# Attention scores as float32 products on row halves, operands placed by GpSimd, in a four-stage network on one core

## Chip, cores and metric

One NeuronCore of a Trainium2 chip. The metric is the device time of one execution in microseconds; less is better. The kernel is a single launch that runs a whole small network on 2048 tokens of 128 features in float32.

## The reference

Four stages run one after the other: a state-space block, a local transformer of two layers, a latent attention, and a mixture of experts, with normalisations between them. The change lies in the latent attention alone:

```python
h = (x - mu) * jax.lax.rsqrt(var + LN_EPS) * ln_scale + ln_bias
c_q = h @ w_down_q.T          # 64 latents
c_kv = h @ w_down_kv.T        # 64 latents
q = (c_q @ w_up_q.T)          # 16 heads of 64, the same for k and v from c_kv
q = _apply_rope_subspace(q, DR)
k = _apply_rope_subspace(k, DR)
scores = jnp.einsum('bhqd,bhkd->bhqk', q, k) * scale
attn = jax.nn.softmax(scores, axis=-1)
out = jnp.einsum('bhqk,bhkd->bhqd', attn, v)
out = out @ w_out.T + residual
```

Every head scores 2048 queries against 2048 keys, each of 64 numbers.

## The kernel before

`latent_attention` works on pairs of heads (8 pairs, `g`), chunks of 512 queries (4, `j`), the two heads of the pair (`w`) and row tiles of 128 queries (4, `r`). One row tile is a 128x2048 block of scores in four PSUM banks (`score`); there are 16 x 16 = 256 of them and one ahead of the loop. The loop body, unrolled for two pairs, runs four times on every engine; nothing but semaphores orders the engines.

TensorE does this for each row tile: the scores of the next row tile (`score_banks`, L1449), banks 0 and 1 once the exponential has read them, then banks 2 and 3; four transposes of probabilities (`turn_tiles`, L1468); in `r == 0` the output products (`output`, L1512); four value products (`mix`, L1500), which alternate between two column halves of the array; four more transposes; and with `w == 0`, `r == 1` and `r == 3`, a piece of the next pair's key and query projection (`pieces`, L1325), whose products alternate between two row halves of the array.

VectorE takes the maximum of each bank (`row_max`, L1479), joins them to `bias` (L1482) and turns half of the probabilities into 32x32 blocks (`turn_blocks`, L1546). ScalarE computes the exponentials, two banks at a time (`exps`, L1487), and copies transposes, outputs and pieces out of PSUM (L1472, L1508, L1520, L1464). SyncE writes the turned blocks to DRAM and reads them back (`write_blocks`, `read_blocks`). GpSimd adds outputs (`add_output`, L1528, L1532) and makes the next pair's operands (`make_parts`).

The scores are made as follows. A float32 number is split into a high part, rounded to the format fp32r, and the rest. `make_parts` multiplies a piece of 256 positions by cosines and sines (L1566), adds the two (L1569), rounds (L1577) and subtracts (L1579). For keys the parts lie in `k_part`, and `send_keys` moves them by four DMAs to `keys`, high parts on rows 0 to 63, low parts on rows 64 to 127. For queries they lie in `q_pair`, and `send_q` (L1339) copies a chunk of one head to both row halves of `q_unit`. Two fp32r passes over all 128 rows then give one bank of scores, one with the high and one with the low part of the queries as stationary operand.

The first pair is made in a block of its own ahead of the loop, from L1349 on: TensorE projects eight pieces of 512, VectorE multiplies (L1427), GpSimd adds (L1386), ScalarE rounds (L1442), VectorE subtracts (L1416), SyncE sends keys (L1371) and queries. In the same block SyncE fills `far` and `bounce` with zeros from `near`.

Of the kernel before, what the change touches and what calls it, by code (L numbers as in the profile page):

```python
# [6 lines left out]
F32 = mybir.dt.float32  # L7
# [1189 lines left out]
def latent_attention(nc, dram, const, x, acc):  # L1197
# [5 lines left out]
    with Space(nc, "g") as sp:  # L1203
# [5 lines left out]
        with Space(nc, "ga") as s:  # L1209
# [11 lines left out]
            with nc.Block() as block:  # L1221
# [71 lines left out]
        k_part = sp.sb("k_part", [P, 2, QH], F32R)  # L1293
# [4 lines left out]
        most = sp.sb("most", [P, 2, 4])  # L1298
        bias = sp.sb("bias", [P, 2])
        sums = sp.sb("sums", [P, 2, RT, 2])  # L1300
        zero = sp.sb("zero", [P, 1])
# [9 lines left out]
             ("w_loaded0", "w_loaded1", "first_full", "first_free", "roped", "high_ready", "low_ready", "k_loaded",  # L1311
              "q_loaded0", "q_loaded1", "score_done", "maxes", "bias_ready", "exp_done", "turn_done", "near_copied",
              "blocks_turned", "written0", "written1", "landed0", "landed1", "mix_done", "mixed_ready", "out_full",
              "out_taken", "added", "piece_full", "piece_taken", "raw_free", "order", "sums_added", "recip_ready",
              "near_read", "zeroed", "values_set", "rescaled")}
        q_loaded = [m["q_loaded0"], m["q_loaded1"]]
# [10 lines left out]
        def send_keys(sync, turn, at, half):  # L1327

            sync.wait_ge(m["low_ready"], PIECES + 2 * half + 1)
            cols = slice(at * QH, (at + 1) * QH)  # L1330
            for head in range(2):
                for part in range(2):
                    sync.dma_start(keys[part * 64:(part + 1) * 64, turn, head, cols].bitcast(F32),
                                   k_part[head * 64:(head + 1) * 64, part].bitcast(F32)).then_inc(m["k_loaded"], 16)

        def send_q(sync, head, chunk):

            for half in range(2):
                sync.dma_start(q_unit[half * 64:(half + 1) * 64, head].bitcast(F32),  # L1339
                               q_pair[head * 64:(head + 1) * 64, :, chunk * QW:(chunk + 1) * QW].bitcast(F32))\  # L1340
                    .then_inc(q_loaded[head], 16)
# [7 lines left out]
        k_first = probs[:, :, 2 * CH:].bitcast(F32R)  # L1349
        with nc.Block() as block:  # L1350

            @block.sync
            def _(sync):
# [13 lines left out]
                for c_ in range(NC):  # L1367
                    sync.wait_ge(m["low_ready"], 2 * c_ + 1)
                    for head in range(2):
                        for part in range(2):  # L1370
                            sync.dma_start(keys[part * 64:(part + 1) * 64, 0, head, c_ * CH:(c_ + 1) * CH].bitcast(F32),  # L1371
                                           k_first[head * 64:(head + 1) * 64, part, c_ % 2 * CH:(c_ % 2 + 1) * CH]
                                           .bitcast(F32)).then_inc(m["k_loaded"], 16)
                sync.wait_ge(m["low_ready"], PIECES)
                for w in range(2):
                    send_q(sync, w, 0)
# [741 lines left out]
```

## Time and profile before

| | us |
|---|---|
| median of 3 runs | 2464.31 (2462.95 to 2468.85) |
| the profiled execution | 2464.99 |
| its span, first to last instruction | 2462.8 |
| TensorE busy | 2126.8 |
| VectorE busy | 1676.6 |
| ScalarE busy | 1381.8 |
| GpSimd busy | 897.5 |

The median is of plain runs; the spans and durations below are of the profiled execution. "PE" is a TensorE product, "PEld" the load of its stationary operand, "DVE" VectorE, "ACT" ScalarE, "POOL" GpSimd, "SP" SyncE. Matmuls are pipelined, so that a row of products lasts longer than the time from its start to the start of the next row; block lengths are read from start to start. A float32 product leaves two records. Duration and start of every row are as recorded; an instruction that waits in the engine's queue is counted from when it runs.

### The profile page before, as it was taken

How to read it: one execution, taken by the hardware profiler on the slowest of the kernel's cores; microseconds unless marked ns; L12 is line 12 of the kernel's file. 1: busy time of each engine (PE TensorE's matmuls, PEld its weight loads, DVE VectorE, ACT ScalarE, POOL GpSimd, SP SyncE). 2: the span in 40 equal slices, each digit the busy share in tenths (PEclk: the TensorE clock that was granted, in tenths of full speed). 3: DMA queues.
4: the chain of work that ended last, by engine and by line, in shares of the span. 5: the costliest groups of instructions: out<-in, count | busy, mean ns of one | idle time of the engine just before them, and what ended most of it. 6: DMA issues, size and time to landing. Idle time of an engine off the chain costs nothing. (4 is left out here: it accounts for less than half of the span.)

```text
span 2462.8 us, 38107 instructions
## 1 busy us (share of the span) xinstructions
PE 2126.8 (86%) x11662; PEld 1309.8 (53%) x11662; DVE 1676.6 (68%) x3033; ACT 1381.8 (56%) x2802; POOL 897.5 (36%) x883
## 2 busy tenths in 40 slices
PE   4745699877984599999999999999999999997397
PEld 2532377435862255556555555555565555553244
DVE  5767766596666477777677777677776777774544
ACT  4233465255630277777677777677776777774121
POOL 0625543264420344443334434344443444433000
PEclk8878899898997699999999999999999999998598
DMA  1001000000001467776677767667776677764100
GB/s 31 1 1 57 1 2 12 20 1 1 2 12 48 154 220 230 239 240 228 215 227 234 247 225 238 211 229 242 233 234 222 222 235 239 232 231 146 36 1 18
DMA packets 224395, 345.61 MB, mean 140 GB/s; under 512 B 16993, under 2 KB 169697, under 8 KB 223905
## 3 DMA queue, kind: packets, MB, share of 16 engines
q1 hardware_dynamic: 224160, 342.86, 42.1%
q8 instruction: 102, 1.67, 0.3%
q14 instruction: 133, 1.08, 0.1%
HBM read 148.55 MB, written 136.31 MB: 116 GB/s over the span
## 5 line engine op out<-in xcount | busy, mean ns | idle before, releaser
L1479 DVE TENSOR_REDUCE g.most<-g_score 128x1 f32<-128x512 f32 x1028 | 639.3, 683 | 342.3 <-PE g_score L1449 341.8
L1487 ACT ACTIVATE g.probs<-g_score,g.bias 128x1024 f32<-128x1024 f32 x514 | 568.0, 1110 | 65.1 <-DVE g.bias L1482 53.7
L1449 PE MATMUL g_score<-g.keys,g.q_unit 128*128 128x512 f32 x2056 | 561.7, 413 | 25.8 <-DMA g.q_unit<-g.q_pair 11.9
L1472 ACT ACTIVATE g.near<-g_turned 128x512 f32<-128x512 f32 x512 | 305.2, 596 | 325.9 <-PE g_turned L1468 325.7
L1449 PEld LDWEIGHTS g_score<-g.keys,g.q_unit 128*128 128x128 f32 x2056 | 361.3, 190 | 145.6 <-ACT g.probs L1487 60.1
L1468 PEld LDWEIGHTS g_turned<-top.ident,g.probs 128*128 128x128 f32 x2048 | 234.1, 140 | 243.2 <-issue 208.1
L1546 DVE STREAM_TRANSPOSE g.blocks<-g.probs 128x1024 f32<-128x1024 f32 x256 | 318.9, 1246 | 31.4 <-DMA bounce<-g.blocks 16.1
L1468 PE MATMUL g_turned<-top.ident,g.probs 128*128 128x128 f32 x2048 | 321.4, 279 | 0.0
L1500 PE MATMUL g_mix_ps<-g.near,mid.y_tok 128*64 128x512 f32 x1056 | 257.4, 609 | 6.3 <-DMA g.far<-bounce 6.3
L1500 PE MATMUL g_mix_ps<-g.far,mid.y_tok 128*64 128x512 f32 x1056 | 255.2, 605 | 0.0
L1566 POOL TENSOR_TENSOR mid.y_tok<-mid.y_tok,g.waves 128x512 f32<-128x512 f32 x128 | 163.7, 1279 | 229.7 <-ACT mid.y_tok L1464 229.7
L1528 POOL TENSOR_TENSOR g.scaled<-g.scaled,g.recip 128x512 f32<-128x512 f32 x67 | 69.7, 1040 | 424.9 <-ACT g.scaled L1520 415.0
L1500 PEld LDWEIGHTS g_mix_ps<-g.near,mid.y_tok 128*64 128x64 f32 x1056 | 64.6, 137 | 103.8 <-issue 96.0
L1500 PEld LDWEIGHTS g_mix_ps<-g.far,mid.y_tok 128*64 128x64 f32 x1056 | 64.3, 136 | 99.4 <-issue 99.4
L1487 ACT ACTIVATION_READ_ACCUMULATOR g.probs<-g_score,g.bias 128x1 f32 x514 | 100.5, 195 | 0.0
L1577 POOL TENSOR_TENSOR g.k_part<-mid.y_tok,g.zero 128x256 fp32r<-128x256 f32 x64 | 39.2, 612 | 161.3 <-DMA g.keys<-g.k_part 154.9
L1569 POOL TENSOR_TENSOR mid.y_tok<-mid.y_tok 128x256 f32<-128x256 f32 x128 | 93.1, 727 | 10.0
L1532 POOL TENSOR_TENSOR top.x_tok<-top.x_tok,g.scaled 128x512 f32<-128x512 f32 x67 | 85.7, 1279 | 5.3
L1464 ACT ACTIVATE mid.y_tok<-g_side 128x512 f32<-128x512 f32 x128 | 77.3, 604 | 1.9
L865 POOL TENSOR_TENSOR lt1.probs<-lt1.probs,lt1.total 128x768 f32<-128x768 f32 x32 | 46.9, 1467 | 71.1 <-DVE lt1.total L920 71.1
L1512 PE MATMUL g_side<-g.mixers,g.mixed 128*128 (+1 forms) x536 | 71.8, 277 | 1.2 <-ACT g.mixed L1508 1.2
L865 POOL TENSOR_TENSOR lt0.probs<-lt0.probs,lt0.total 128x768 f32<-128x768 f32 x32 | 46.9, 1467 | 70.9 <-DVE lt0.total L920 70.9
(358 smaller groups left out, 3235.6 us busy)
## 6 DMA issues: line engine op xcount, KB each, us to landing
bounce<-g.blocks SPq DMA_DIRECT2D x256, 512.0 KB, 5.2
g.far<-bounce SPq DMA_DIRECT2D x256, 512.0 KB, 4.4
g.q_unit<-g.q_pair SPq DMA_DIRECT2D x132, 256.0 KB, 4.4
g.keys<-g.k_part SPq DMA_DIRECT2D x256, 64.0 KB, 3.5
g.far<-g.near SPq DMA_DIRECT2D x8, 512.0 KB, 5.5
lt.turns<-turns SPq DMA_DIRECT2D x1, 2048.0 KB, 8.1
g.waves<-g_waves SPq DMA_DIRECT2D x1, 2048.0 KB, 10.2
g.keys<-g.probs SPq DMA_DIRECT2D x16, 128.0 KB, 2.4
```

The source lines that it names most:

```text
L865: nc.gpsimd.tensor_tensor(p, p, total[:, slot].unsqueeze(2).broadcast_to([P, HH, KEYS]), ALU.mult).then_inc(m["probs_ready"], 1)
L1449: ins = nc.tensor.matmul(score[:, b], q[:, part], k_of(b), start=(part == 0), stop=(part == 1))
L1464: nc.scalar.activation(raw[:, kind], side[:, kind], ACT.Copy).then_inc(m["piece_taken"], 1)
L1468: ins = nc.tensor.transpose(turned[:, k * P:(k + 1) * P], probs[:, r % 2, t * P:(t + 1) * P], ident[:])
L1472: nc.scalar.activation(near[:, w, tiles, r * P:(r + 1) * P], turned[:].rearrange("p (t n) -> p t n", n=P), ACT.Copy).then_inc(m["near_copi ...
L1479: nc.vector.tensor_reduce(most[:, slot, k:k + 1], score[:, k], AX.X, ALU.max, negate=True)\
L1487: nc.scalar.activation(probs[:, slot, k * 2 * CH:(k + 1) * 2 * CH], score[:, 2 * k:2 * k + 2].rearrange("p b n -> p (b n)"), ACT.Exp, bias ...
L1500: ins = nc.tensor.matmul(out, values[:, t], moving, start=(t < 2), stop=(t >= T - 2))
L1532: nc.gpsimd.tensor_tensor(a, a, scaled[:], ALU.add).then_inc(m["added"], 1)
L1546: nc.vector.transpose(blocks[:, r % 2].rearrange("p j t c -> p t j c"), probs[:, r % 2, NEAR * P:].rearrange("p (t j a) -> p t j a", j=4, ...
L1566: nc.gpsimd.tensor_tensor(both, both, waves[:, at].rearrange("p s n -> p (s n)"), ALU.mult)\
L1569: nc.gpsimd.tensor_tensor(total, total, both[:, QH:], ALU.add).then_inc(m["order"], 1)
```

## The change

The score product becomes a float32 product over 64 rows. `keys` holds the key blocks 0 and 2 of a head on rows 0 to 63 and the blocks 1 and 3 on rows 64 to 127; `queries` holds each head's queries on both row halves, for this pair and the next. One row tile's scores are two pairs of products, one product of a pair on each row half. `make_parts` no longer splits: it multiplies, and then adds cosine and sine part straight into the place where TensorE reads them, on 64 rows at a time, with a shift by 64 rows where needed: two additions for a piece of keys, four for a piece of queries. All DMAs of keys and queries go, with `send_keys`, `send_q`, `q_loaded` and `k_loaded`. TensorE waits for the operands of the next pair once in a pair, for the last of its 16 pieces. `row_max` takes one maximum over two banks in place of one for each bank. In the first block VectorE adds the keys into place and GpSimd the queries; ScalarE has nothing to do there.

```diff
-        keys = sp.sb("keys", [P, 2, 2, S], F32R)
-        q_pair = sp.sb("q_pair", [P, 2, S], F32R)
-        q_unit = sp.sb("q_unit", [P, 2, 2, QW], F32R)
+        keys = sp.sb("keys", [P, 2, 2, S // 2])
+        queries = sp.sb("queries", [P, 2, 2, S])
...
+        def place_keys(engine, turn, head, at, width, first, second):
+
+            block, inside = divmod(at * width, CH)
+            cols = slice(block // 2 * CH + inside, block // 2 * CH + inside + width)
+            return engine.tensor_tensor(keys[block % 2 * 64:block % 2 * 64 + 64, turn, head, cols],
+                                        first[head * 64:head * 64 + 64], second[head * 64:head * 64 + 64], ALU.add)
+
+        def place_queries(engine, turn, head, half, at, width, first, second):
+
+            return engine.tensor_tensor(queries[half * 64:half * 64 + 64, turn, head, at * width:(at + 1) * width],
+                                        first[head * 64:head * 64 + 64], second[head * 64:head * 64 + 64], ALU.add)
...
-                for n in range(PIECES):
-                    pool.wait_ge(m["first_free"], 2 * n + 2)
-                    nc.gpsimd.tensor_tensor(cos_part[:, n % 2], cos_part[:, n % 2], sin_part[:, n % 2], ALU.add)\
-                        .then_inc(m["roped"], 1)
-                nc.gpsimd.memset(zero[:], 0.0)
+                for c_ in range(NC):
+                    pool.wait_ge(m["first_free"], 4 * c_ + 4)
+                    for crossed in range(2):
+                        pool.wait_ge(m["zeroed"], 1 + 4 * c_ + 2 * crossed)
+                        for head in range(2):
+                            place_queries(nc.gpsimd, 0, head, head ^ crossed, c_, CH, cos_part[:, 1], sin_part[:, 1])\
+                                .then_inc(m["zeroed"], 1)
+                    pool.wait_ge(m["zeroed"], 5 + 4 * c_)
+                    pool.sem_inc(m["q_first"], 1)
...
+                    if kind == 0:
+                        dve.wait_ge(m["first_free"], 2 * n + 2)
+                        for head in range(2):
+                            ins = place_keys(nc.vector, 0, head, c_, CH, cos_part[:, 0], sin_part[:, 0])
+                        ins.then_inc(m["k_first"], 1)
...
-        def score_banks(pe, banks, q, k_of):
-
-            for b in banks:
-                for part in range(2):
-                    ins = nc.tensor.matmul(score[:, b], q[:, part], k_of(b), start=(part == 0), stop=(part == 1))
-                ins.then_inc(m["score_done"], 1)
+        def score_pair(pe, pair, turn, head, chunk, r):
+
+            cols = slice(chunk * QW + r * P, chunk * QW + (r + 1) * P)
+            for odd in range(2):
+                rows = slice(odd * 64, odd * 64 + 64)
+                nc.tensor.matmul(score[:, 2 * pair + odd], queries[rows, turn, head, cols],
+                                 keys[rows, turn, head, pair * CH:(pair + 1) * CH], start=True, stop=True)\
+                    .then_inc(m["score_done"], 1)
...
-            for k in range(4):
-                dve.wait_ge(m["score_done"], 4 * before + k + 1)
-                nc.vector.tensor_reduce(most[:, slot, k:k + 1], score[:, k], AX.X, ALU.max, negate=True)\
-                    .then_inc(m["maxes"], 1)
+            for k in range(2):
+                dve.wait_ge(m["score_done"], 4 * before + 2 * k + 2)
+                nc.vector.tensor_reduce(most[:, slot, k:k + 1], score[:, 2 * k:2 * k + 2].rearrange("p b n -> p (b n)"),
+                                        AX.X, ALU.max, negate=True).then_inc(m["maxes"], 1)
...
             nc.gpsimd.tensor_tensor(both, both, waves[:, at].rearrange("p s n -> p (s n)"), ALU.mult)\
                 .then_inc(m["order"], 1)
             pool.wait_ge(m["order"], n + 1)
...
+            if kind == 0:
+                for head in range(2):
+                    place_keys(nc.gpsimd, turn, head, at, QH, first, second).then_inc(m["order"], 1)
+                    pool.wait_ge(m["order"], n + 2 + head)
             else:
+                for crossed in range(2):
+                    for head in range(2):
+                        place_queries(nc.gpsimd, turn, head, head ^ crossed, at, QH, first, second)\
+                            .then_inc(m["order"], 1)
+                    pool.wait_ge(m["order"], n + 3 + 2 * crossed)
+            pool.sem_inc(m["parts_ready"], 1)
...
                                         if w == 1 and j == NC - 1:
                                             on = 1 - turn
-                                            pe.wait_ge(m["k_loaded"], 256 + 512 * (g + 1))
+                                            pe.wait_ge(m["parts_ready"], 16 * (g + 1) + 2)
```

## Rows read from the trace of the kernel before

**Rows 1.** The page: busy time, share of the span and instructions of each engine

```profile
PE 2126.8 (86%) x11662; PEld 1309.8 (53%) x11662; DVE 1676.6 (68%) x3033; ACT 1381.8 (56%) x2802; POOL 897.5 (36%) x883
```

**Rows 2.** Stretches: length, busy time (instructions) of PE, PEld, DVE, ACT, POOL, clock, DMA

```profile
1000.00:1400.00 400.00, 395.57 (x2060) 235.30 (x2058) 290.58 (x475) 286.72 (x514) 166.54 (x186) 0.99 0.70 231
...
1480.88:1523.79 42.91, 42.91 (x227) 25.37 (x225) 31.84 (x52) 31.32 (x57) 18.02 (x21) 1.00 0.70 233
```

**Rows 3.** Waits in 860 to 2260: us in total, times, longest us

```profile
PEld g_score L1449 <- ACT g.probs L1487: 58.6, 190, 0.9
...
PE g_score L1449 <- DMA g.keys<-g.k_part: 0.8, 2, 0.4
```

**Rows 4.** Timeline of TensorE: start us, us, what, shapes, records

```profile
1506.49 0.66 PE L1468 MATMUL g_turned<-top.ident,g.probs 128*128 128x128 f32 x4
1506.90 2.10 PE L1449 MATMUL g_score<-g.keys,g.q_unit 128*128 128x512 f32 x8
1508.84 0.60 PE L1468 MATMUL g_turned<-top.ident,g.probs 128*128 128x128 f32 x4
1509.36 1.94 PE L1500 MATMUL g_mix_ps<-g.far,mid.y_tok 128*64 128x512 f32 x8
1511.23 0.66 PE L1468 MATMUL g_turned<-top.ident,g.probs 128*128 128x128 f32 x4
1511.82 1.14 PE L1325 MATMUL g_side<-g.c,g.w_up 64*128 64x256 f32 x8
1512.88 2.12 PE L1449 MATMUL g_score<-g.keys,g.q_unit 128*128 128x512 f32 x8
1514.84 0.60 PE L1468 MATMUL g_turned<-top.ident,g.probs 128*128 128x128 f32 x4
```

**Rows 5.** Timeline of VectorE and ScalarE behind the scores that start at 1506.90

```profile
1507.64 2.48 DVE L1479 TENSOR_REDUCE g.most<-g_score 128x1 f32<-128x512 f32 x4 [1.84 <-PE g_score L1449]
...
1510.35 1.11 ACT L1487 ACTIVATE g.probs<-g_score,g.bias 128x1024 f32<-128x1024 f32 x1 [0.29 <-DVE g.bias L1482]
1511.37 0.19 ACT L1487 ACTIVATION_READ_ACCUMULATOR g.probs<-g_score,g.bias 128x1 f32 x1
1511.46 1.10 ACT L1487 ACTIVATE g.probs<-g_score,g.bias 128x1024 f32<-128x1024 f32 x1
```

**Rows 6.** Timeline of TensorE, window 1511.80 to 1511.83 alone

```profile
1511.82 0.49 PE L1325 MATMUL g_side<-g.c,g.w_up 64*128 64x256 f32 x2
```

**Rows 7.** Timeline of all engines around the third row tile of a unit

```profile
1491.28 2.26 PE L1449 MATMUL g_score<-g.keys,g.q_unit 128*128 128x512 f32 x8
...
1492.65 0.60 ACT L1464 ACTIVATE mid.y_tok<-g_side 128x512 f32<-128x512 f32 x1
1493.34 1.27 POOL L1566 TENSOR_TENSOR mid.y_tok<-mid.y_tok,g.waves 128x512 f32<-128x512 f32 x1 [0.39 <-ACT mid.y_tok L1464]
1493.38 0.60 PE L1468 MATMUL g_turned<-top.ident,g.probs 128*128 128x128 f32 x4
```

**Rows 8.** Groups by form: what, shapes, count, busy us, mean ns of one, idle before

```profile
L1566 POOL TENSOR_TENSOR mid.y_tok<-mid.y_tok,g.waves 128x512 f32<-128x512 f32 x128 | 163.7, 1279 | 229.7 <-ACT mid.y_tok L1464 229.7
L1569 POOL TENSOR_TENSOR mid.y_tok<-mid.y_tok 128x256 f32<-128x256 f32 x128 | 93.1, 727 | 10.0
...
L707 DVE TENSOR_REDUCE la1.inverse<-lp1.square 128x16 f32<-128x1024 f32 x16 | 19.2, 1200 | 0.0
```

**Rows 9.** Timeline of the block that makes the first pair

```profile
807.39 1.89 DVE L1427 TENSOR_TENSOR g.probs<-g_score,g.waves 128x512 f32<-128x512 f32 x3 [0.94 <-PE g_score L1325]
808.44 2.49 POOL L1386 TENSOR_TENSOR g.probs<-g.probs 128x512 f32<-128x512 f32 x2
...
812.88 1.64 POOL L1386 TENSOR_TENSOR g.probs<-g.probs 128x512 f32<-128x512 f32 x1 [1.95 <-DVE g.probs L1427]
...
845.59 3.66 PE L1449 MATMUL g_score<-g.keys,g.q_unit 128*128 128x512 f32 x8 [11.86 <-DMA g.q_unit<-g.q_pair]
```

**Rows 10.** Timeline of TensorE at the loop's jump, one of three

```profile
1548.61 3.68 PE L1449 MATMUL g_score<-g.keys,g.q_unit 128*128 128x512 f32 x8 [3.88 <-issue]
```

More of the change, by code:

```diff
@@ L1325, in projected @@
             return nc.tensor.matmul(out, w_up[rows, turn, swap * P:(swap + 1) * P], c[rows, cols], start=True, stop=True)
[L1327 to L1331, printed above, removed]
-                for part in range(2):
[L1333 to L1341, printed above, removed]
+        def place_keys(engine, turn, head, at, width, first, second):
[6 more added lines that the diff above has]
+                                        first[head * 64:head * 64 + 64], second[head * 64:head * 64 + 64], ALU.add)
         def load_w(sync, turn, pair):
@@ L1366, in _ @@
                                    [:, 0:4 * RUN]).then_inc(written[w], 16)
[L1367 to L1376, printed above, removed]
                 for w in range(2):
@@ L1430, in _ @@
                             .then_inc(m["first_free"], 1)
-                    if n:
-                        rest(n - 1)
-                rest(PIECES - 1)
-            @block.scalar
-            def _(act):
-                for n in range(PIECES):
-                    kind, c_ = n % 2, n // 2
-                    act.wait_ge(m["roped"], n + 1)
-                    if kind == 0 and c_:
-                        act.wait_ge(m["k_loaded"], 64 * c_)
-                    nc.scalar.activation(first_part(n, 0), cos_part[:, n % 2], ACT.Copy)\
-                        .then_inc(m["high_ready"], 1)
-        def score_banks(pe, banks, q, k_of):
-            for b in banks:
-                for part in range(2):
-                    ins = nc.tensor.matmul(score[:, b], q[:, part], k_of(b), start=(part == 0), stop=(part == 1))
-                ins.then_inc(m["score_done"], 1)
+                    if kind == 0:
[10 more added lines that the diff above has]
+                    .then_inc(m["score_done"], 1)
         def pieces(pe, turn, at):
@@ L1461, in take_piece @@
         def take_piece(act, half, kind):
-            act.wait_ge(m["raw_free"], 2 * half + 1 + kind)
+            act.wait_ge(m["parts_ready"], 2 * half + 1 + kind)
             act.wait_ge(m["piece_full"], 2 * half + 1 + kind)
@@ L1558, in read_blocks, with make_parts @@
                            bounce[4 * w + r].rearrange("(i p x) -> p i x", i=4, p=P)).then_inc(landed[w], 16)
-        def make_parts(pool, g, j, at, half, kind):
-            n = 3 * (2 * half + kind)
+        def make_parts(pool, turn, at, half, kind):
             both = raw[:, kind]
-            total = both[:, 0:QH]
+            first, second = both[:, 0:QH], both[:, QH:]
+            n = 8 * half + 3 * kind
             pool.wait_ge(m["piece_taken"], 2 * half + 2 + kind)
@@ L1622, in _ @@
                 pool.sem_inc(m["added"], 1)
[L1623 removed]
+                pool.sem_inc(m["parts_ready"], 2)
                 with pool.Fori(0, PAIRS_G // 2) as i:
@@ L1641, in _ @@
             def _(pe):
-                pe.wait_ge(q_loaded[0], 32)
-                pe.wait_ge(m["k_loaded"], 256)
-                score_banks(pe, range(4), q_unit[:, 0, :, 0:P], lambda b: keys[:, 0, 0, b * CH:(b + 1) * CH])
+                for k in range(2):
+                    score_pair(pe, k, 0, 0, 0, 0)
                 mix(pe, 0, range(0, 4))
```

75 lines of the change are left out of this document (18 added, 57 removed).

## The prediction

> **What bounds the kernel now.** I read the page's engine line first [rows 1]: TensorE is busy for 86% of the span, the other engines for 68% and less. A share is an average, so the stages came next [rows 2]. In the latent attention loop TensorE is busy 395.6 of 400 us at a granted clock of 0.99, VectorE 291, ScalarE 287, GpSimd 167. The reader is to see two things there: the loop is TensorE's, and the DMA share of 0.70 is large but belongs to an engine set that nobody waits for. The waits confirm that [rows 3]: in 1400 us TensorE waits 0.8 us for the key transfers that the change removes, and its weight loads wait 58.6 us in 190 pieces for the exponentials. So the transfers are hidden, the softmax chain is nearly as long as TensorE's own work, and what counts is how long TensorE's blocks are [rows 4] and how much slack the chain behind them leaves [rows 5].
>
> The unit of the count is a row tile: scores of the next 128 queries, four transposes, four value products ("mix"), four transposes; every fourth has four output products, every fourth a projection of key and query pieces. Eight row tiles take 42.91 us [rows 2]; there are 32 such groups.
>
> **Scores on TensorE: a loss of 28 us.** Before, eight passes of 512 columns over all rows take 1.94 us after transposes, 1.96 us after a projection [rows 4]. After, four float32 products on row halves. The trace shows such products: the projection block is eight records on 64 rows and 256 columns in 1.06 us, the mix block eight records on column halves and 512 columns in 1.87 us [rows 4]. The difference is 0.81 us for four times 256 columns, 0.20 each, which at 2.4 GHz fits two passes for each record (2 x 256 / 2.4 = 0.213 us) with two records running side by side; in a window of 30 ns at the start of a projection two records run [rows 6]. So a score block is four steps of 0.427 = 1.71 us, plus what entering and leaving the row halves costs. That is 1.06 - 4 x 0.213 = 0.21 us in the projection block (0.16 in the mix block). Score block after: 1.92 us, 0.02 less than before. The array now changes its form on both sides of it, though, and the neighbours show that price: transposes in front of a projection take 0.59 us where those in front of today's scores take 0.41 (+0.17, unrounded), and transposes between two changes take 0.59 where those with one take 0.52 (+0.06). Per plain row tile: -0.02 + 0.17 + 0.06 = +0.21 us. The two of eight whose scores follow a projection share its form: projection and scores together were 1.06 + 1.96 = 3.02, now 12 half steps of 0.213 plus one 0.21 = 2.77, so -0.25 + 0.06 = -0.19. Eight row tiles: 6 x 0.21 - 2 x 0.19 = +0.88 us; times 32: +28 us.
>
> **The softmax chain: +4 us.** Today the first maximum starts 0.74 us after the scores do, four of them end at 3.22, the exponential starts at 3.45 and its second half ends near 5.66 [rows 5]; then the next scores' second half may start. A plain row tile is 1.94 + 0.52 + 1.87 + 0.41 = 4.74 us, so the next scores' first half (free at about 4.71) fits, and the second half is just late: three score blocks of eight take about 2.10 (one stands in [rows 7]: 1491.28 to 1493.38), one start is 0.14 late, some 0.65 us per eight. After: the first pair is ready 1.15 us after the start (0.10 entry, 0.427, last product 0.59), the maximum runs over 1024 columns. No row has that over PSUM; a reduction of 1024 columns from SBUF took 1.20 us [rows 8], two of today's take 2 x 0.60 + 0.08 = 1.28 [rows 5]. I take 1.21, near the first since it is one instruction. The second maximum starts at 1.15 + 1.13 = 2.28 and ends at 3.49, the exponential starts at 3.72, and the scores behind it may start at 4.98 and 6.08, against 4.95 and 5.91 for TensorE. So plain row tiles wait 0.03 + 0.14, and a weight load that must wait is no longer hidden (+0.1): 0.27 us, and the row tile after it has caught up. With an output or projection between them there is 1 us of slack (the longer block hides it). Three of eight: 0.80 us, minus the 0.65 of today: +0.15, times 32 = about +4 us. The bounds: at 1.20 nothing changes; at 1.36 (two of today's 0.68 end to end) the chain is 0.30 longer, each of four plain row tiles waits 0.33 + 0.24: +1.5 us per eight, +48 us in all. In favour: if the chain is shorter than I think by 0.2 us, no wait is left, -26 us against the sum.
>
> **Placement on GpSimd, end of a head pair: +7 us.** make_parts loses an addition, a rounding and a subtraction on 128 rows and gets two additions on 64 rows for keys, four for queries. The nearest row is an addition of 128x256 in 0.73 us [rows 8]; fewer rows give fewer lanes, not fewer elements in each, so I take 0.73 apiece. A query piece costs 1.28 + 4 x 0.73 + waits of 0.08 each = 4.3 us, a key piece 2.9, against 3.4 both today: 19 us of GpSimd in 44, still no bound. But before, the queries of the next pair had four units of time and only keys were waited for; now the first score of a pair waits for the last piece, a query piece. ScalarE hands it over 1.98 us after the scores of the third row tile began, GpSimd starts at 2.06 [rows 7] and would end at 6.5, where TensorE arrives at 4.95 + 0.24. Behind that wait on TensorE's queue stand all its transposes and mixes; VectorE and ScalarE have nothing else to do. 1.3 us x 8 pairs = 10.4, minus the 0.8 of today's key waits and the 0.27 that those row tiles no longer wait: +7 us. Bounds: 0 if two additions on opposite row halves run side by side (then 2.8 us for the piece); 8 x 2.5 = 20 if a shift by 64 rows makes an addition 1.3 times longer.
>
> **First pair: -6 us.** Now keys and queries leave by DMA and the first scores start at 845.59, released by the last query transfer [rows 9]. After, each chunk is four multiplications (0.60 apart) and two key additions on VectorE, then four query additions of 512 on GpSimd (1.22 apart, two in 2.49 [rows 9]); the query buffer is single, so GpSimd's 5.3 us and the next two multiplications (1.3 us) alternate. GpSimd can start when VectorE has done 807.39 plus three further pairs of steps, about 810.8; four rounds of 7.1 us less the last multiplications end at about 837.6, three memsets 0.7, 0.9 to the next block: 839.2, 6 us earlier. VectorE's additions run beside GpSimd's and may lengthen them (today 1.64 instead of 1.27 when both work): in the 5.3 + 0.4. If the halves run side by side, a round is 2.6 + 0.1 + 1.3 = 4.0 us, about as long as VectorE's own six steps: 827, 18 us earlier.
>
> **What costs and gains nothing.** The q and k transfers and their waits on SyncE's queue go; the block transfers behind them then land sooner, but TensorE waits for one only after the loop. VectorE does two maxima for four (-0.3 us per row tile): it sat idle. The three 4 us pauses at the loop's own jump [rows 10] stay. The Trainium skill (TensorE: Matmul & The Clock Gate, What overlaps and what doesn't) says that matmuls start strictly in program order. Each float32 product is two records, so by that rule the odd half could only begin beside the even half's second record; that is five steps for four, and is the fourth rival below. The mix block speaks against it: five steps of 0.427 would be 2.13 us and it takes 1.87. The skill's GPSIMD Engine Reference (Instruction dispatch) says that a core of GpSimd starts the next instruction when its own share is done; by that rule the additions on opposite halves would overlap, the first rival. No operation on 64 rows stands in this trace.
>
> **Sum.** Profiled execution 2464.99 us (span 2462.8), 0.7 above the median of 2464.31. +28 + 4 + 7 - 6 = +33: 2498 us.
>
> **Rivals.**
> 1. GpSimd's halves run side by side: pair ends cost -1 instead of +7, the start gives 18 instead of 6: 28 + 4 - 1 - 18 = +13, 2478 us. For: independent row halves without a wait between; against: back-to-back additions overlap by only 0.05 us now. Chance 0.22.
> 2. The chain is longer, above all the wide maximum (1.36): +33 + 48, 2546 us. Against: one instruction was never dearer than two halves in this trace. 0.07.
> 3. Faster than before: the change of form costs nothing on both sides of the scores. A score block is 1.71 and a plain row tile 4.53, but the chain then binds at 4.88. Four plain row tiles: 19.5 against 19.3 today; the other four 22.2 against 23.6: -1.2 per eight, -38 us; with -6 and +11 it is 2432 us. It decides from a change price below about 0.1 us in place of 0.4. Against: the projection block pays the price on both sides [rows 4]. 0.04.
> 4. Row halves do not overlap as the mix's column halves do: five steps, +0.43 us x 257 = +110: 2608 us; not at all, +1.7 us x 257, 2930 us. 0.05 together.
> 5. The chain's slack is better than worked out and GpSimd's halves overlap: 13 - 26 = -13 at best, around no change (2455 to 2472). 0.09.
> My own case, 2484 to 2525 us: 0.53.
>
> **Chances and range.** A measurement of this kernel tells about 0.3% (7 us) from no change. Faster by more: 0.06 (rival 3 and a part of 5); within: 0.09; slower: 0.85. The range takes in my case, rival 1 and half of 5: 2464 to 2532.
>
> **What would show it.** The score line with eight records of 64x512 in pairs, block 1.92 us; transposes in front of it 0.59; maxima x514 of about 1.2 us; idle time of the first score block of each pair ended by GpSimd; loop groups of eight at 43.9; the first scores near 839. I am wrong if the score records do not pair, if transposes in front stay at 0.41, or if the maximum is far from 1.21.

## The result and the profile after

The changed kernel takes 2506.02 us (median; 2500.34 to 2509.63) against 2466.15 for the kernel before in the same comparison: a ratio of 1.0157, 95% interval 1.0141 to 1.0173. It is slower by 1.6%, as forecast; the forecast of 2498 is 8 us short. The profiled execution took 2504.55 us with a span of 2502.8, 40.0 longer than before's 2462.8.

The page of the kernel after, its line of engines and the groups that the change touches (busy us, mean ns of one, idle time before it and who ended it):

```profile
PE 2165.8 (87%) x11662; PEld 1109.1 (44%) x11662; DVE 1627.4 (65%) x2519; ACT 1369.2 (55%) x2794; POOL 919.4 (37%) x890
...
L1445 DVE TENSOR_REDUCE g.most<-g_score 128x1 f32<-128x1024 f32 x514 | 605.7, 1220 | 468.5 <-PE g_score L1414 468.4
...
L1414 PE MATMUL g_score<-g.keys,g.queries 64*128 64x512 f32 x2056 | 531.2, 623 | 34.0 <-POOLq L1545 11.9
...
L1331 POOL TENSOR_TENSOR g.queries<-mid.y_tok 64x256 f32<-64x256 f32 x256 | 185.1, 723 | 19.7
```

TensorE is still the busiest engine by far. The maximum over 1024 columns takes 1.22 us. The scores are records on 64 rows, eight for a block (2056 in all). A placing addition takes 0.723 us.

TensorE's timeline of the kernel after (start us, us, what, shapes, records; its durations overlap by a little, so blocks are counted from start to start):

```profile
1524.77 1.99 PE L1414 MATMUL g_score<-g.keys,g.queries 64*128 64x512 f32 x8
1526.69 0.66 PE L1434 MATMUL g_turned<-top.ident,g.probs 128*128 128x128 f32 x4
1527.27 1.94 PE L1466 MATMUL g_mix_ps<-g.far,mid.y_tok 128*64 128x512 f32 x8
1529.14 0.66 PE L1434 MATMUL g_turned<-top.ident,g.probs 128*128 128x128 f32 x4
1529.73 1.13 PE L1320 MATMUL g_side<-g.c,g.w_up 64*128 64x256 f32 x8
1530.70 1.88 PE L1414 MATMUL g_score<-g.keys,g.queries 64*128 64x512 f32 x8
1532.51 0.66 PE L1434 MATMUL g_turned<-top.ident,g.probs 128*128 128x128 f32 x4
...
1535.64 2.23 PE L1414 MATMUL g_score<-g.keys,g.queries 64*128 64x512 f32 x8
```

A score block is 1.92 us (1524.77 to 1526.69), the transposes behind it 0.58, the mix 1.87, the transposes ahead of the next form change 0.59: 4.96 for a plain row tile without a wait, against 4.74 in [rows 4]. Projection and scores together are 2.78 (1529.73 to 1532.51), against 3.02. The block at 1535.64 stands for those that wait for the exponential inside: 2.15.

The softmax chain of one row tile, and the scores it holds back:

```profile
1503.41 1.99 PE L1414 MATMUL g_score<-g.keys,g.queries 64*128 64x512 f32 x8
...
1504.61 2.35 DVE L1445 TENSOR_REDUCE g.most<-g_score 128x1 f32<-128x1024 f32 x2 [2.00 <-PE g_score L1414]
...
1507.19 1.12 ACT L1453 ACTIVATE g.probs<-g_score,g.bias 128x1024 f32<-128x1024 f32 x1 [0.57 <-DVE g.bias L1448]
...
1508.45 0.30 PEld L1414 LDWEIGHTS g_score<-g.keys,g.queries 64*128 64x128 f32 x4 [0.25 <-ACT g.probs L1453]
```

The first maximum starts 1.20 us after the scores, the exponential at 3.78, the next scores at 5.04 where TensorE would be there at 4.96.

The waits of 860 to 2260 us (us in total, times, longest), the stretch of [rows 3], and eight row tiles and the middle of the loop as stretches (length, busy time of PE, PEld, DVE, ACT, POOL, clock, DMA share, GB/s):

```profile
PEld g_score L1414 <- ACT g.probs L1453: 136.6, 296, 1.7
```

```profile
1503.41:1547.56 44.15, 44.12 (x226) 19.18 (x225) 30.11 (x36) 31.08 (x57) 18.37 (x20) 1.00 0.56 191
1000.00:2100.00 1100.00, 1079.36 (x5472) 470.67 (x5472) 734.32 (x879) 759.02 (x1369) 451.93 (x493) 1.00 0.54 188
```

The 58.6 us and 190 waits of before have become 136.6 and 296, and 42.91 us for eight row tiles have become 44.15 [rows 2]. The transfers are gone (DMA share 0.56 for 0.70), and TensorE got nothing for it (experiment 10).

The end of a head pair, one of eight, with the last query piece on GpSimd:

```profile
1552.60 2.22 PE L1414 MATMUL g_score<-g.keys,g.queries 64*128 64x512 f32 x8
...
1556.04 3.12 POOL L1331 TENSOR_TENSOR g.queries<-mid.y_tok 64x256 f32<-64x256 f32 x4
...
1559.35 1.13 PE L1414 MATMUL g_score<-g.keys,g.queries 64*128 64x512 f32 x4 [1.49 <-POOLq L1545]
```

TensorE's own waits in the loop, 840 to 2290 us:

```profile
PE g_score L1414 <- POOLq L1545: 11.9, 8, 1.5
...
PE g_score L1414 <- issue: 9.5, 3, 4.2
```

And the first pair, one of its four rounds and the first scores:

```profile
810.79 5.96 POOL L1331 TENSOR_TENSOR g.queries<-g.probs 64x512 f32<-64x512 f32 x4 [2.41 <-DVE g.probs L1399]
...
811.94 2.36 DVE L1326 TENSOR_TENSOR g.keys<-g.probs 64x512 f32<-64x512 f32 x2
...
839.38 3.37 PE L1414 MATMUL g_score<-g.keys,g.queries 64*128 64x512 f32 x8 [10.72 <-PEq L1340]
```

**Where the 40.0 us are.** The first block: 839.38 for 845.59 [rows 9], -6.2. The eights: 32 x (44.15 - 42.91) = +39.7. The pair ends: 8 waits of 1.49 = +11.9, of which the row tiles around them take back about 0.5. The loop's three jumps, from the last transposition's start to the first scores': 4.43 + 2.95 + 2.90 us for 4.23 + 4.15 + 3.97, -2.1. After the second and third jump the clock did not fall, and the first score block took 1.92 us and not 3.5: -3.2. The one wait for a block transfer behind the loop: -1.1. What is left, which no term explains: +1.5. Sum 40.

### The profile page after: what moved, and what is told of

Same layout as the page of the kernel before. It is cut to its first block and busy times, and to the rows that moved or that the text cites. A ratio compares the mean times of both kernels' runs of the same rounds, so it can differ in the third digit from the quotient of the medians.

```text
span 2502.8 us, 36315 instructions
## 1 busy us (share of the span) xinstructions
PE 2165.8 (87%) x11662; PEld 1109.1 (44%) x11662; DVE 1627.4 (65%) x2519; ACT 1369.2 (55%) x2794; POOL 919.4 (37%) x890
## 5 line engine op out<-in xcount | busy, mean ns | idle before, releaser
L1445 DVE TENSOR_REDUCE g.most<-g_score 128x1 f32<-128x1024 f32 x514 | 605.7, 1220 | 468.5 <-PE g_score L1414 468.4
L1414 PE MATMUL g_score<-g.keys,g.queries 64*128 64x512 f32 x2056 | 531.2, 623 | 34.0 <-POOLq L1545 11.9
L1434 PEld LDWEIGHTS g_turned<-top.ident,g.probs 128*128 128x128 f32 x2048 | 215.0, 141 | 402.5 <-issue 314.6
L1434 PE MATMUL g_turned<-top.ident,g.probs 128*128 128x128 f32 x2048 | 336.6, 287 | 0.0
L1414 PEld LDWEIGHTS g_score<-g.keys,g.queries 64*128 64x128 f32 x2056 | 173.6, 186 | 232.8 <-ACT g.probs L1453 142.3
L1331 POOL TENSOR_TENSOR g.queries<-mid.y_tok 64x256 f32<-64x256 f32 x256 | 185.1, 723 | 19.7
L1466 PEld LDWEIGHTS g_mix_ps<-g.near,mid.y_tok 128*64 128x64 f32 x1056 | 64.6, 136 | 102.7 <-issue 94.9
L1326 POOL TENSOR_TENSOR g.keys<-mid.y_tok 64x256 f32<-64x256 f32 x128 | 92.5, 723 | 10.0
L1320 PE MATMUL g_side<-g.c,g.w_up 64*128 64x256 f32 x512 | 72.6, 402 | 0.0
```

The lines of the kernel that those rows point to most:

```text
L1326: return engine.tensor_tensor(keys[block % 2 * 64:block % 2 * 64 + 64, turn, head, cols], first[head * 64:head * 64 + 64], second[head * 6 ...
L1331: return engine.tensor_tensor(queries[half * 64:half * 64 + 64, turn, head, at * width:(at + 1) * width], first[head * 64:head * 64 + 64], ...
L1414: nc.tensor.matmul(score[:, 2 * pair + odd], queries[rows, turn, head, cols], keys[rows, turn, head, pair * CH:(pair + 1) * CH], start=Tru ...
L1434: ins = nc.tensor.transpose(turned[:, k * P:(k + 1) * P], probs[:, r % 2, t * P:(t + 1) * P], ident[:])
L1445: nc.vector.tensor_reduce(most[:, slot, k:k + 1], score[:, 2 * k:2 * k + 2].rearrange("p b n -> p (b n)"), AX.X, ALU.max, negate=True).the ...
L1466: ins = nc.tensor.matmul(out, values[:, t], moving, start=(t < 2), stop=(t >= T - 2))
```

## The experiments

All comparisons are with the kernel before, run on the same chip; a ratio stands with its 95% interval. Where two changed kernels are set side by side by their medians, a few us are open: the kernel before had medians from 2466.15 to 2468.77 us in these comparisons.

**1. GpSimd's wait taken from the pair end.** TensorE waits for the last piece one row tile later, at the start of the next pair. That piece holds queries of the fourth chunk, which are needed three chunks on.

```
 on = 1 - turn
-pe.wait_ge(m["parts_ready"], 16 * (g + 1) + 2)
+pe.wait_ge(m["parts_ready"], 16 * (g + 1) + 1)
...
+if j == 0 and w == 0 and r == 0:
+    pe.wait_ge(m["parts_ready"], 16 * g + 2)
```

> The changed kernel, but at the end of a head pair TensorE waits for all pieces except the last one (queries of chunk 3, needed three chunks later); for that one it waits at the start of the next pair. Theory (GpSimd's last four additions stop TensorE once in a pair): the eight waits of 1.5 us go, the three short waits of the softmax chain that they absorbed come back, so 2506 - 12 + 2 = about 2496 us, ratio to before about 1.012. Rival (the wait only covers one that the exponentials would cause anyway): 2506 us, and eight waits of the same length with another releaser.

Measured: 2497.09 us, 1.0117 (1.0100 to 1.0133), 9 us less than after (28 above its own kernel before, where after was 40 above). The waits for GpSimd are gone from the loop, and what is left among TensorE's waits (840 to 2290 us) is the loop's own jump:

```profile
PE g_score L1414 <- issue: 11.5, 3, 3.9
```

So the pair ends cost about what the account above gives them. The pauses at the jumps rose by 2 us (9.5 to 11.5), which took back a part of the 11.9 us.

**2. The chain made shorter.** Each of the two maxima reads only the first of its two banks, so it takes about half the time, and the bias is no longer the true row maximum. TensorE's work is untouched.

```
-nc.vector.tensor_reduce(most[:, slot, k:k + 1], score[:, 2 * k:2 * k + 2].rearrange("p b n -> p (b n)"),
+nc.vector.tensor_reduce(most[:, slot, k:k + 1], score[:, 2 * k],
```

> The changed kernel, but each maximum is taken over the first of its two banks alone (512 of 1024 columns), after both are ready; the bias is then no longer the true row maximum. It shortens the chain behind the scores by 1.1 us (0.53 for each maximum) and leaves TensorE's work as it is. Theory (the chain costs 0.96 us per eight row tiles, the rest of the loss is TensorE's own blocks): eight row tiles fall from 44.15 to 43.15 us, 32 x 1.0 = 31 us less, the GpSimd wait at the pair ends grows by 2: about 2477 us, ratio 1.005. Rival (the wide maximum and the chain are the whole loss): back to 2466 or below. Rival (the chain is hidden): 2506.

Measured: 2471.73 us, 1.0011 (1.0000 to 1.0022). The waits of 860 to 2260 us, and a stretch of eight row tiles (length, busy time of each engine, clock, DMA share, GB/s):

```profile
PEld g_score L1414 <- ACT g.probs L1453: 38.2, 124, 1.4
```

```profile
1401.79:1444.98 43.19, 43.19 (x226) 19.53 (x225) 22.52 (x36) 30.56 (x56) 18.40 (x20) 1.00 0.58 195
```

34 us go with the chain by the medians (of 40 us above its own kernel before, 3 are left), although TensorE's work is instruction for instruction that of the kernel after. The first reading, that the chain alone made the kernel slower, would be wrong: the kernel before has chain waits too, 0.65 us in eight row tiles, or 21 us in all. Without them TensorE's blocks are 42.91 - 0.65 = 42.26 us for eight before, and 43.19 here, so the blocks' own growth is 0.93 x 32 = 30 us, for 28 in the sum. What goes is the chain's part of after, (44.15 - 43.19) x 32 = 31 us, and 3 us at the pair ends, where the wait for GpSimd fell from 11.9 to 9.0 (it was expected to grow by 2). The two costs add up: 30 of blocks, and 31 (after) less 21 (before) of chain.

**3. One pass at lower precision.** Keys and queries are rounded to fp32r; the rest of the change is as it was, row halves and placing included.

```
-keys = sp.sb("keys", [P, 2, 2, S // 2])
-queries = sp.sb("queries", [P, 2, 2, S])
+keys = sp.sb("keys", [P, 2, 2, S // 2], F32R)
+queries = sp.sb("queries", [P, 2, 2, S], F32R)
```

> The changed kernel with keys and queries stored as fp32r, so that a score product is one pass at reduced precision instead of four; row halves and placement stay. Theory (the price at the borders of the score block is that of changing between whole array and row halves, whatever the number format): transposes ahead of the scores stay at 0.59 us and those behind at 0.585, the block itself falls from 1.92 to 0.21 + 4 x 0.21 = 1.06 plus waits. Then the chain binds: a plain row tile takes 4.6 to 4.75 us, one with output or pieces 5.0, eight about 38.7, so 32 x 5.4 = 173 us less: 2320 to 2360 us. Rival (the price belongs to float32 products): transposes ahead fall to 0.41.

Measured: 2334.26 us, 0.9454 (0.9438 to 0.9470): 5.5% faster than the kernel before and the fastest of this study, at a lower precision of the scores. Its timeline of TensorE:

```profile
1507.67 0.66 PE L1434 MATMUL g_turned<-top.ident,g.probs 128*128 128x128 f32 x4
1508.26 0.50 PE L1414 MATMUL g_score<-g.keys,g.queries 64*128 64x512 f32 x2
1509.35 0.50 PE L1414 MATMUL g_score<-g.keys,g.queries 64*128 64x512 f32 x2 [0.59 <-ACT g.probs L1453]
1509.84 0.66 PE L1434 MATMUL g_turned<-top.ident,g.probs 128*128 128x128 f32 x4
1510.43 1.94 PE L1466 MATMUL g_mix_ps<-g.far,mid.y_tok 128*64 128x512 f32 x8
```

The transposes ahead of the scores are 0.59 us (1507.67 to 1508.26) and those behind 0.59 (1509.84 to 1510.43) here too. So row halves have this price without float32 as well. The scores now wait for the exponential between their two halves: TensorE no longer binds.

**4. Each product over all 128 rows.** A bank then holds the sum of two key blocks' scores, which is not what the reference asks for.

```
-nc.tensor.matmul(score[:, 2 * pair + odd], queries[rows, turn, head, cols],
-                 keys[rows, turn, head, pair * CH:(pair + 1) * CH], start=True, stop=True)\
+nc.tensor.matmul(score[:, 2 * pair + odd], queries[:, turn, head, cols],
+                 keys[:, turn, head, pair * CH:(pair + 1) * CH], start=True, stop=True)\
```

> The changed kernel with each score product over all 128 rows of keys and queries in float32, so that a bank holds the sum of two key blocks' scores: no longer the scores of the reference. No row halves, no side by side. Theory (form change): the block takes 8 x 0.427 = 3.42 us, transposes ahead of it 0.41, behind it 0.53; eight row tiles 54.1, so 32 x 9.9 - 12 = about 300 us more: 2810 us. It also gives what the row halves are worth. Rival (the price belongs to float32 products): transposes ahead stay at 0.59, behind at 0.585.

Measured: 2855.46 us in one execution, 45 above the forecast. TensorE's timeline:

```profile
1643.15 3.70 PE L1414 MATMUL g_score<-g.keys,g.queries 128*128 128x512 f32 x8
1646.69 0.60 PE L1434 MATMUL g_turned<-top.ident,g.probs 128*128 128x128 f32 x4
1647.22 1.94 PE L1466 MATMUL g_mix_ps<-g.far,mid.y_tok 128*64 128x512 f32 x8
1649.09 0.66 PE L1434 MATMUL g_turned<-top.ident,g.probs 128*128 128x128 f32 x4
1649.60 3.70 PE L1414 MATMUL g_score<-g.keys,g.queries 128*128 128x512 f32 x8
```

Eight records now follow one another, 3.54 us for 1.92 (8 x 0.427 = 3.42, and 0.12): the row halves run side by side, and that saves 1.62 us a block. In this form, still float32, the transposes behind the scores fall from 0.58 to 0.53 and those ahead from 0.59 to 0.51. That is the control for the form's price in float32: 0.05 behind and 0.08 ahead. The forecast for those ahead was 0.41, as in the kernel before; they stay 0.10 longer than that, although no row half is in use, so a part of what the change added ahead of the scores is not the row halves' alone. These 0.10 us and the 0.12 in the block, each in six of eight row tiles, are the 1.3 us by which eight row tiles took more than the forecast (55.4, from the score block at 1643.15 to the one at 1698.55, for 54.1): 42 of the extra 45 us. A row tile of 6.45 us holds no wait for the chain.

**5. Four maxima in the kernel after.**

```
-for k in range(2):
-    dve.wait_ge(m["score_done"], 4 * before + 2 * k + 2)
-    nc.vector.tensor_reduce(most[:, slot, k:k + 1], score[:, 2 * k:2 * k + 2].rearrange("p b n -> p (b n)"),
...
+for k in range(4):
+    dve.wait_ge(m["score_done"], 4 * before + k + 1)
+    nc.vector.tensor_reduce(most[:, slot, k:k + 1], score[:, k], AX.X, ALU.max, negate=True)\
...
```

> The changed kernel with one maximum for each bank, as before the change, in place of one for two banks. Both banks of a pair are ready at once, so there is nothing to start earlier. Theory (the wide maximum is not a cause of the loss): the four end 3.68 us after the scores start instead of 3.55, the chain is 0.13 longer, four plain row tiles of eight wait for it: 32 x 0.5 = 16 us more, about 2522 us, ratio 1.023. Rival (joining the maxima made the chain longer and is a part of the loss): 2500 us or below.

Measured: 2512.48 us, 1.0176 (1.0156 to 1.0196), 6 above after, where the intervals of the ratios overlap, and 10 below the forecast. The chain of one row tile, whose scores start at 1505.21:

```profile
1506.37 2.48 DVE L1445 TENSOR_REDUCE g.most<-g_score 128x1 f32<-128x512 f32 x4 [1.87 <-PE g_score L1414]
```

The first maximum starts 1.16 us after the scores, only 0.04 before a wide one; the four take 2.48 for 2.35. In this form the wide maxima are no cause of the loss. At best they gain a few us, which these intervals don't tell from nothing.

**6. Two wide maxima in the kernel before.** The reverse edit, alone.

```
-for k in range(4):
-    dve.wait_ge(m["score_done"], 4 * before + k + 1)
-    nc.vector.tensor_reduce(most[:, slot, k:k + 1], score[:, k], AX.X, ALU.max, negate=True)\
...
+for k in range(2):
+    dve.wait_ge(m["score_done"], 4 * before + 2 * k + 2)
+    nc.vector.tensor_reduce(most[:, slot, k:k + 1], score[:, 2 * k:2 * k + 2].rearrange("p b n -> p (b n)"),
...
```

> The kernel before with one thing of the change, the maximum over two banks. There the banks come one after the other, and the wide maximum must wait for the second. Theory (the chain has next to no slack before): it ends at 3.56 us instead of 3.22 after the scores start, plain row tiles go from 4.74 to about 5.05 with stalls of 0.2 in the middle: 1.4 us per eight, 45 us in all, 2505 to 2515 us. Rival (the chain has slack before, as TensorE's waits of 1 us in all suggest): 2466 us.

Measured: 2502.33 us, 1.0135 (1.0116 to 1.0154), 34 us slower. From its timeline:

```profile
1506.28 2.29 PE L1449 MATMUL g_score<-g.keys,g.q_unit 128*128 128x512 f32 x8
...
1507.52 2.36 DVE L1479 TENSOR_REDUCE g.most<-g_score 128x1 f32<-128x1024 f32 x2 [1.36 <-PE g_score L1449]
...
1511.36 0.96 PE L1449 MATMUL g_score<-g.keys,g.q_unit 128*128 128x512 f32 x3
```

The maximum now starts at 1.24 where the first of four started at 0.74 [rows 5], and a plain row tile is 5.08 (1506.28 to 1511.36) for 4.74. Here a longer chain shows at once: with four banks filled one behind another, a maximum of each as it ends is what keeps the chain short. The same edit is a loss of 34 us in one form and none in the other.

**7. One pass in the kernel before.** The product of the queries' low part is left out, the form, the transfers and the maxima stay.

```
-for part in range(2):
-    ins = nc.tensor.matmul(score[:, b], q[:, part], k_of(b), start=(part == 0), stop=(part == 1))
+ins = nc.tensor.matmul(score[:, b], q[:, 0], k_of(b), start=True, stop=True)
```

> The kernel before with one of its two fp32r passes for each bank: the low part of the queries is still made and sent but left out of the scores, which lowers their precision. The whole array is kept, so there is no change of form, and the transfers stay. Theory (at four passes the softmax chain binds instead of TensorE, in both forms): score block 0.94 us, transposes ahead 0.41; the chain sets plain row tiles to 4.6 to 4.7, the ones with output 4.7, with pieces 4.85; eight 37.7 against 38.2 in the single-pass kernel on row halves (2334 us): 2300 to 2330 us. Rival (transfers of keys and queries bind once TensorE is faster): above 2340, with TensorE waiting for them.

Measured: 2420.39 us, 0.9806 (0.9787 to 0.9826): 90 us above the range of the forecast, on the rival's side. Its waits of 840 to 2290 us, and from the page (idle time of the block transposition behind the bar):

```profile
PE g_score L1448 <- ACT g.probs L1486: 94.9, 188, 2.5
...
PE g_score L1448 <- DMA g.keys<-g.k_part: 15.2, 8, 2.5
```

```profile
L1545 DVE STREAM_TRANSPOSE g.blocks<-g.probs 128x1024 f32<-128x1024 f32 x256 | 318.8, 1245 | 105.5 <-DMA bounce<-g.blocks 96.4
```

TensorE has less to do, but it does not get there: it waits 94.9 us for exponentials. VectorE waits 96.4 us for the block buffers' transfers to leave (16.1 in the kernel before), the maxima stand behind it on its queue, and the key transfers are waited for too. That points to the transfers once TensorE is quicker; this kernel also differs from experiment 3 in its maxima and its form, so experiment 9 puts it to the test.

**8. Experiments 1 and 3 together.**

```
+keys = sp.sb("keys", [P, 2, 2, S // 2], F32R)
...
+pe.wait_ge(m["parts_ready"], 16 * (g + 1) + 1)
...
```

> Single-pass fp32r scores on row halves together with the earlier wait at the end of a pair: the two edits of the runs before in one. TensorE waited 16.5 us for GpSimd in the single-pass kernel. Theory (independent places): 2334 - 16.5 + about 3 = 2320 us. Rival (behind that wait stands the softmax chain, which then binds there too): 2330 us or more.

Measured: 2344.19 us, 0.9488 (0.9463 to 0.9513), not better than 3 but 10 us slower. Its waits of TensorE, 840 to 2290 us:

```profile
PE g_score L1414 <- ACT g.probs L1453: 108.5, 213, 2.4
...
PE g_score L1414 <- issue: 15.7, 3, 6.0
```

Experiment 3 had 16.5 us of waits for GpSimd, 99.8 for the exponentials and no more than 2.9 us at a jump. The 16.5 are gone; 8.7 came back in front of the exponentials, and the pauses at the jumps rose from 5.7 us (two) to 15.7 (three), the longest 6.0. Removing a wait in a loop that TensorE does not bind gained nothing, and why the jumps grew was not found.

**9. Experiment 3 with the old transfers back.** Transfers of the old number and size run at the old places of the queue, from `c` into tiles that nobody reads.

```
...
 write_blocks(sync, w, 0, G)
+if w == 1:
+    sync.wait_ge(dk_loaded, 64 * (H + 2))
+    move_keys(sync)
...
 write_blocks(sync, w, 3, G + 3)
+if w == 0:
+    sync.wait_ge(dk_loaded, 64 * (H + 1))
+    move_keys(sync)
+sync.wait_ge(dq_loaded[w], 32 * (4 * g + j + 1))
+move_q(sync, w)
 read_blocks(sync, w, 3, G + 3)
...
```

> The single-pass kernel on row halves, with transfers of the old kernel's sizes and number put back (two of 256 KB for each unit, four of 64 KB for each piece of keys), at the old places in SyncE's queue, into tiles that nobody reads. They wait for nothing but their own predecessor. Theory (with TensorE out of the way the transfers of keys and queries cost time by delaying the block transfers, on which VectorE's transposes wait; this is why the one-pass kernel with transfers took 2420 us and not 2330): VectorE's waits for the block transfers rise from 50 us towards 96, the time from 2334 to between 2365 and 2400 us. Rival (the one-pass kernel is slower for another reason, such as its waits for keys and the maxima by bank): 2334 to 2345 us.

Measured: 2420.24 us, 0.9800 (0.9784 to 0.9817): 86 us slower than experiment 3, 20 above the forecast, and level with experiment 7, whose scores are one pass as well and whose transfers are real. A piece of SyncE's queue, and the stretch of 1000 to 2100 us, first of this kernel and then of experiment 3:

```profile
1501.68 2.93 SPq L1350 DMA_DIRECT2D g.dummy_k<-g.c  x4
1504.73 1.17 SPq L1342 DMA_DIRECT2D g.dummy_q<-g.c  x2
1506.25 0.55 SPq L1542 DMA_DIRECT2D g.far<-bounce  x1
```

```profile
1000.00:2100.00 1100.00, 964.10 (x4968) 465.14 (x4964) 787.93 (x931) 799.85 (x1449) 474.94 (x517) 0.94 0.73 236
```

```profile
1000.00:2100.00 1100.00, 993.20 (x5346) 470.29 (x5344) 844.06 (x1001) 861.86 (x1556) 510.54 (x555) 0.99 0.64 214
```

Six small transfers keep SyncE's queue for 4.6 us (1501.68 to 1506.25), and the block transfers stand behind them. So the queue is a way by which they can cost; the load on the DMA engines (a share of 0.73 for 0.64) is another, and no run here separates the two. TensorE's granted clock was also lower, 0.94 for 0.99, so a part of the 86 us can be a slower TensorE. That part was not measured; in experiment 7, which took the same time, the clock of this stretch was 0.98. The idle time of the block transposition before a block buffer is free rose from 50.5 us (experiment 3) to 88.5.

**10. The kernel after with the old transfers back**, the same edit on the changed kernel.

```
...
+if w == 1:
+    sync.wait_ge(dk_loaded, 64 * (H + 2))
+    move_keys(sync)
...
```

> The changed kernel with the same transfers put back. Theory (in the float32 form TensorE binds and the transfers are hidden, so that their removal gained nothing): 2506 us, at most 2512. Rival (their removal gained something, and the loss by the scores is larger than it looks): 2520 us or more.

Measured: 2503.14 us, 1.0145 (1.0128 to 1.0162), no loss against after (2506.02), with the DMA share back at 0.69. Its waits for the exponentials in 860 to 2260 us:

```profile
PEld g_score L1433 <- ACT g.probs L1472: 136.5, 296, 1.7
```

That is the 136.6 and 296 of the kernel after. In the float32 form the transfers are hidden entirely.

## Why the prediction was right, and where it was off

**Transfers hidden, TensorE binds: right.** Experiment 10 puts them back at no cost, as [rows 3] said with 0.8 us. The claim holds for this length of TensorE's blocks only: in experiments 3, 7 and 9 the same transfers are worth 86 us.

**TensorE's blocks, +28: right.** Said 1.92, 0.59 ahead, 2.77 for projection and scores; measured 1.92, 0.59 and 2.78. A plain row tile is +0.22 for +0.21. Experiment 2, without most chain waits, is the test: 42.91 - 0.65 + 0.88 = 43.14 us for eight follow from the terms, and 43.19 were measured. Experiments 3 and 4 show whose price it is, with one limit. In fp32r, row halves cost the transposes ahead 0.18 us (0.59 for 0.41) and those behind 0.06; in float32 they cost 0.08 and 0.05, since float32 products on full rows have 0.51 ahead of them and not 0.41. The prediction gave the whole 0.17 ahead to the change of form. The total of 0.59 was right, but by experiment 4 about 0.10 of it comes without row halves; what makes it was not found.

**Four steps of product pairs, not five: right.** The block of 1.92 us has four steps, and in the first 30 ns of the block at 1524.77 two records already run. The Trainium skill (TensorE: Matmul & The Clock Gate, What overlaps and what doesn't) gives a strict order of starts. The prediction counted five steps from it by taking the two records of a product as neighbours in that order, and that count is what the block contradicts. The rule itself is not tested: the trace doesn't say to which product a record belongs.

**The softmax chain, +4: mechanism right, size short.** The wide maximum was 1.22 for 1.21. But the first one starts at 1.20 for 1.15, and all behind it is as much later: the exponential at 3.78 for 3.72, the next scores at 5.04 for 4.98. Three of eight wait 0.24 in the block (0.27 said), and smaller waits that the sum had at nothing (0.08 in a fourth block, and 0.08 and 0.09 ahead of the blocks at 1508.45 and 1535.64) make it 0.96 for eight in place of 0.80. So the chain is +0.31 in eight and +10 us in all; with the 30 of the blocks the eights cost 39.7 where 28 + 4 was said. 44.15 was measured where 43.9 follows from the terms. This was the term that was sized too small: the first maximum's start. Its terms (0.10 + 0.427 + 0.59) give 1.12 us, and the trace has the end of the first pair's records at 1.13; the prediction left 0.03 for the hand-over to VectorE, and it took 0.07, at a point where nothing of the chain was slack.

**Pair ends, +7: right in kind, short by 4.** The wait was there in all 8 pairs, 1.49 us each where 1.3 was said, and the row tiles around it took back 0.5 in all. Four placing additions took 3.12 us, one behind another: rival 1 is out. Experiment 1 confirms the term from the other side, with 9 us by the medians.

**The first pair, -6: right**, 6.2. A round was 7.4 us for 7.1 (GpSimd's four additions 5.96 beside VectorE's two, 5.25 alone), so that the last addition ended at 838.28 for 837.6. The memsets and the way to the first scores then took 1.1 us and not 1.6. The two errors cancel, and that is luck.

**The loop's jumps, 0: wrong, and in favour.** Two of three were 1.2 us shorter with no fall of the clock behind them: -5 us. Nothing in the trace of before pointed to it, and in experiment 1 they are back at 4.0 us and more. Its cause is open; the last section has what the runs show of it.

**The sum.** The errors were +8 (eights), +4 (pair ends), -5 (jumps), -1 and +1 (the wait behind the loop, the rest): +7 net, for a span that grew by 40.0 where 33 was said. Part of the closeness is thus two errors that cancel. Three of the prediction's own sums are slightly off, by about 1 us each at most: the chain's 0.15 x 32 is 4.8 and not 4, the last query piece ends at 2.06 + 4.3 = 6.4 and not 6.5 by its terms, and four rounds from 810.8 end at 837.9 and not 837.6.

**The rivals.** Rival 2 (chain longer by its maximum) did not happen, since 1.22 is far from 1.36; its place was right all the same: experiment 6 shows how a later maximum costs 34 us in the kernel before. Rival 3 (a free form change) is denied by the transposes of 0.59. Rival 4 is denied by the block's length. Rival 5 needed additions side by side. Of the experiments' forecasts, 7 missed most widely, by 90 us (4 missed by 45, 8 by 24, 9 by 20, 5 by 10): there I took [rows 3] to say that the transfers are hidden in general, when it says so only of a TensorE that is as slow as it is.

## What to carry to other kernels

Where a chain of other engines is nearly as long as the bound engine's own blocks, a small change in when its first input is ready counts in each turn: here 0.05 us later than worked out made 0.16 us in eight row tiles. Work out that start with the hand-over in it, and keep a row for it. A hidden transfer is hidden from the present bound only: before counting on a faster engine, put the same transfers beside the faster form, as in experiments 3 and 9. And an edit that is a loss in one form (wide maxima, 34 us) can be even in another, so parts of a change must be tried each in the form it is for.

## What the runs showed of the hardware

- GpSimd's additions on opposite row halves never overlapped: 0.723 us each, four in 3.12 us, and the busy time of all 256 (185.1 us) is 256 times the 0.723. The Trainium skill (GPSIMD Engine Reference, Instruction dispatch) lets a core start the next instruction when its own share is done; no gain of that kind shows here. Halving the rows saved nothing: 128 rows of 256 columns take 0.727 [rows 8].
- VectorE and GpSimd, adding from SBUF at the same time, slow each other: in the first pair two of VectorE's 64x512 additions take 1.38 us alone and 2.36 beside GpSimd, and GpSimd's four take 5.25 alone and 5.96 beside VectorE.
- The pause of TensorE at the loop's jump is not fixed. It was 2.9 to 4.4 us in the kernel after, and the clock behind it either fell or stayed. The first jump and the second, and 4 us from each (clock is the last but two):

```profile
1205.98 3.79 PE L1414 MATMUL g_score<-g.keys,g.queries 64*128 64x512 f32 x8 [4.16 <-issue]
...
1567.06 1.99 PE L1414 MATMUL g_score<-g.keys,g.queries 64*128 64x512 f32 x8 [2.68 <-issue]
```

```profile
1205.98:1209.98 4.00, 4.00 (x10) 1.48 (x11) 1.37 (x2) 0.00 (x0) 0.00 (x0) 0.50 0.40 138
1567.06:1571.06 4.00, 4.00 (x24) 2.37 (x26) 2.72 (x4) 0.82 (x2) 0.00 (x0) 1.00 0.52 199
```

A granted clock of 0.50 is 1.2 GHz, 1.00 is 2.4 GHz, and the same eight records take 3.79 and 1.99 us.

The idle time at the jumps goes with the wait for GpSimd in the row tile before it. Where TensorE waits 1.1 to 1.5 us there (after, experiments 2, 5 and 10), eleven of twelve pauses were 2.6 to 3.1 us and one 4.2; where it doesn't (the kernel before, experiments 1 and 6), all nine were 3.7 to 5.2. So a part of what experiment 1 took away before the jump came back at it. This is seen side by side and not shown as a cause: experiment 9 has the wait and pauses of 3.5 to 5.1, experiment 4 has next to none (1.0 us in all) and pauses of 2.4 to 3.9.
